# Attention scores on the two row halves of TensorE

## The reference

```
x = x + 0.5 * _L0_ffn_ref(_layernorm(x), ...)
x = x + _L0_attn_ref(_layernorm(x), ...)          # a state-space block
x = x + 0.5 * _L0_ffn_ref(_layernorm(x), ...)
x = x + 0.5 * _L1_ffn_ref(_layernorm(x), ...)     # routed
x = x + _L1_attn_ref(_layernorm(x), ...)          # here
x = x + 0.5 * _L1_ffn_ref(_layernorm(x), ...)

# _L1_attn_ref: NH, NKV = 32, 8 heads of HD = 16
q, k = _apply_rope(q, cos, sin), _apply_rope(k, cos, sin)
k, v = jnp.repeat(k, 4, axis=1), jnp.repeat(v, 4, axis=1)
logits = jnp.einsum('bhqd,bhkd->bhqk', q, k) / 4.0
logits = jnp.where(causal, logits, finfo.min)
out = jnp.einsum('bhqk,bhkd->bhqd', softmax(logits), v)
return out.transpose(0, 2, 1, 3).reshape(...) @ Wo.T
```

## Time and profile before

| | us |
|---|---|
| median of 3 runs | 2516.3 |
| lowest, highest | 2514.64, 2520.89 |
| profiled execution | 2520.89 |
| its span | 2519.0 |
| PE, DVE, ACT, POOL busy | 2371.8, 1661.3, 1313.1, 1329.8 |
| attention in the span | about 2098 to 2453 |
| of it main loop | 2238 to 2440 |

### The profile page before, as it was taken

The page is one execution under the profiler, slowest core; times in us unless marked ns, Lnnn a source line. Parts: engine busy times, 40 slices in busy tenths (PEclk is TensorE's granted clock), DMA queues, the critical chain, the costliest instruction groups (busy, mean ns, idle before and its releaser), DMA issues. The chain is left out here.

```text
span 2519.0 us, 32506 instructions
## 1 busy us (share of the span) xinstructions
PE 2371.8 (94%) x12122; PEld 1833.6 (73%) x12122; DVE 1661.3 (66%) x2163; ACT 1313.1 (52%) x1902; POOL 1329.8 (53%) x875
## 2 busy tenths in 40 slices
PE   6997899999999999999999999999889986989986
PEld 5876688888888888888888888888668753565643
DVE  5555887687588588588578678678365535674424
ACT  2323576477477467467467567567423223325533
POOL 2221498599499499589579679669622200000000
PEclk9998999999999999999999999999889998989997
DMA  4321333233233233233233323323134202000001
GB/s 128 97 80 46 115 110 105 89 96 119 79 111 115 80 104 103 93 100 114 88 102 109 92 89 117 98 95 102 46 84 97 90 14 78 1 2 2 2 1 47
DMA packets 163260, 203.98 MB, mean 81 GB/s; under 512 B 24380, under 2 KB 86080, under 8 KB 162976
## 3 DMA queue, kind: packets, MB, share of 16 engines
q1 hardware_dynamic: 163104, 201.90, 26.3%
HBM read 198.37 MB, written 3.15 MB: 80 GB/s over the span
## 5 line engine op out<-in xcount | busy, mean ns | idle before, releaser
L1892 POOL TENSOR_TENSOR mamba_w_lo<-mamba_raw,mamba_w_hi 128x512 fp32r<-128x512 f32 x272 | 436.1, 1613 | 289.9 <-ACT mamba_w_hi L1720 289.9
L76 PE MATMUL psum<-mamba_hT_lo,mamba_w_hi 128*128 128x512 f32 x1152 | 461.7, 401 | 5.6 <-DVE mamba_bc L1983 3.0
L77 PE MATMUL psum<-mamba_hT_hi,mamba_w_hi 128*128 128x512 f32 x1152 | 456.2, 396 | 0.0
L78 PE MATMUL psum<-mamba_hT_hi,mamba_w_lo 128*128 128x512 f32 x1152 | 456.1, 396 | 0.0
L1911 POOL TENSOR_SCALAR mamba_L<-mamba_A,mamba_ts 128x256 f32<-128x256 f32 (+1 forms) x256 | 334.3, 1320 | 0.1
L2015 DVE TENSOR_TENSOR mamba_L<-mamba_L,mamba_cb 128x1536 f32<-128x1536 f32 x128 | 302.0, 2359 | 22.2 <-ACT mamba_L L1769 16.5
L76 PEld LDWEIGHTS psum<-mamba_hT_lo,mamba_w_hi 128*128 128x128 f32 x1152 | 217.0, 188 | 55.9 <-DVE mamba_bc L1983 3.3
L1983 DVE SCALAR_TENSOR_TENSOR mamba_hid<-psum,mamba_cw,mamba_hid 128x1022 f32<-128x1022 f32 (+2 forms) x192 | 245.1, 1277 | 18.0 <-ACT mamba_hid L1727 13.5
L78 PEld LDWEIGHTS psum<-mamba_hT_hi,mamba_w_lo 128*128 128x128 f32 x1152 | 216.9, 188 | 52.4
L77 PEld LDWEIGHTS psum<-mamba_hT_hi,mamba_w_hi 128*128 128x128 f32 x1152 | 216.9, 188 | 49.1
L2042 DVE SCALAR_TENSOR_TENSOR mamba_zs_lo<-mamba_z,mamba_dgn,mamba_zs_hi 128x512 fp32r<-128x512 f32 x128 | 117.6, 923 | 172.0 <-ACT mamba_zs_hi L1792 172.0
(11 more groups left out here) (278 smaller groups left out, 5002.7 us busy)
## 6 DMA issues: line engine op xcount, KB each, us to landing
mamba_A<-mamba_a_dram SPq DMA_DIRECT2D x128, 512.0 KB, 4.4
mamba_raw<-in_win SPq DMA_DIRECT2D x144, 256.0 KB, 2.6
mamba_raw<-in_wout SPq DMA_DIRECT2D x128, 256.0 KB, 2.6
mamba_Eb<-mamba_e_dram SPq DMA_DIRECT2D x128, 128.0 KB, 3.0
ffn_raw<-in_w SPq DMA_DIRECT2D x80, 128.0 KB, 3.5
ffn_scl<-in_s SPq DMA_DIRECT2D x80, 128.0 KB, 3.7
ffn_scl<-in_s SPq DMA_DIRECT2D x86, 64.0 KB, 2.3
ffn_raw<-in_w SPq DMA_DIRECT2D x20, 256.0 KB, 2.6
```

The lines of the kernel that those rows point to most:

```text
L76: e.matmul(out, wh, ml, start=start, stop=False)
L77: e.matmul(out, wh, mh, start=False, stop=False)
L78: return e.matmul(out, wl, mh, start=False, stop=stop)
L1892: e.tensor_tensor(w.lo[:, k % NSPLIT, :], raw[:, k % NRAW, :], w.hi_read[:, k % NSPLIT, :], ALU.subtract).then_inc(s["w_lo"], 1)
```

## The change

Both score products now contract over 64 rows at a time. `HALVES` names the two halves of the partitions. In `score` the matmul of head h reads rows 64 h to 64 h + 63 of the q stack and of its k stack. The mask is brought in halves too: `halfm[:, n, :]` holds the mask's rows 64 n to 64 n + 63 on both halves of the partitions, and `shifted` is an identity of 64 columns with zeros on both sides, so that a window of 128 columns puts these rows in the right place; four mask matmuls stand where two stood. `score_t(t, m)` computes two key heads, one on each half, into banks 4 and 5, with four mask matmuls of 256 columns on the diagonal, waits until both banks are free, and signals once; units follow in two shares and not in four. Making the new tables takes a memset, a second DMA and three more casts.

```
-                for i in range(4 if t < TQ else 0):
-                    score_t(t, i)
-                    for k in range(i * len(units) // 4, (i + 1) * len(units) // 4):
+                for m in range(2 if t < TQ else 0):
+                    score_t(t, m)
+                    for k in range(m * len(units) // 2, (m + 1) * len(units) // 2):
                         score(*units[k])
```

```
 # score
                     for h in range(2):
-                        e.matmul(psum[:, 2 * (k % 2) + h, 0:n], qs[:, b, z, qt * P:(qt + 1) * P],
-                                 ks[:, b, 2 * (z // QPK) + h, 0:n], start=True, stop=False)
-                    for h in range(2):
-                        last = e.matmul(psum[:, 2 * (k % 2) + h, n - P:n], identr[:], maskr[:], start=False, stop=True)
+                        e.matmul(psum[:, 2 * (k % 2) + h, 0:n], qs[HALVES[h], b, z, qt * P:(qt + 1) * P],
+                                 ks[HALVES[h], b, 2 * (z // QPK) + h, 0:n], start=True, stop=False)
+                    for j in range(2):
+                        for h in range(2):
+                            last = e.matmul(psum[:, 2 * (k % 2) + h, n - P:n],
+                                            shifted[HALVES[h], P // 2 * (1 - j):P // 2 * (1 - j) + P],
+                                            halfm[HALVES[h], j, :], start=False, stop=j == 1)
 # score_t
-                    kv, k = 4 * j + i, 4 * t + i
-                    if k >= 2:
-                        e.wait_ge(exped, k - 1)
+                    k = 4 * t + 2 * m
+                    if k:
+                        e.wait_ge(exped, k)
...
-                    last = e.matmul(out, ks[:, b, kv, kt * P:(kt + 1) * P], q, start=True, stop=kt < qt)
-                    if kt == qt:
-                        last = e.matmul(out, maskr[:], identr[:, :].unsqueeze(1).to_broadcast([P, QPK, P]),
-                                        start=False, stop=True)
+                    for h in range(2):
+                        last = e.matmul(outs[h], ks[HALVES[h], b, 4 * j + 2 * m + h, kt * P:(kt + 1) * P],
+                                        qs[HALVES[h], b, z:z + QPK, qt * P:(qt + 1) * P], start=True, stop=kt < qt)
+                    for n in range(2 if kt == qt else 0):
+                        for h in range(2):
+                            last = e.matmul(outs[h][:, :, HALVES[n]], halfm[HALVES[h], n, :],
+                                            identr[HALVES[h], HALVES[h]].unsqueeze(1).to_broadcast([P // 2, QPK, P // 2]),
+                                            start=False, stop=n == 1)
 # convert (ScalarE)
                 e.wait_ge(sel_cut, 2)
+                e.wait_ge(zeros_set, 1)
...
-                e.copy(maskr[:], cmask[:]).then_inc(mask_ready, 1)
+                e.copy(halfm[:], hmask[:]).then_inc(mask_ready, 1)
                 e.copy(identr[:], ident[:]).then_inc(mask_ready, 1)
+                e.copy(shifted[:], zeros[:]).then_inc(mask_ready, 1)
+                e.wait_ge(mask_ready, 3)
+                for h in HALVES:
+                    e.copy(shifted[h, P // 2:P], ident[h, h]).then_inc(mask_ready, 1)
```

More of the change, by code:

```diff
@@ L842, in attention @@
     ROWS, ONE, SPARE = 32, AHD, 48
+    HALVES = (slice(0, P // 2), slice(P // 2, P))
     SCALE = AHD ** -0.5
@@ L854, in attention @@
         cos, sin, rot = c.sb("cos", [P, SEQ]), c.sb("sin", [P, SEQ]), c.sb("rot", [P, P])
-        cmask = c.sb("cmask", [P, P])
-        maskr, identr = c.sb("maskr", [P, P], F32R), c.sb("identr", [P, P], F32R)
+        hmask = c.sb("hmask", [P, 2, P])
+        identr = c.sb("identr", [P, P], F32R)
+        halfm = c.sb("halfm", [P, 2, P], F32R)
+        shifted = c.sb("shifted", [P, P + P // 2], F32R)
+        zeros = c.sb("zeros", [P, P + P // 2])
         sel = c.sb("sel", [P, 2, QPK + NKV, P], F32R)
-        w_in, sel_in, sel_cut, sel_ready, mask_ready = (c.sem(s) for s in (
-            "w_in", "sel_in", "sel_cut", "sel_ready", "mask_ready"))
+        w_in, sel_in, sel_cut, sel_ready, mask_ready, zeros_set = (c.sem(s) for s in (
+            "w_in", "sel_in", "sel_cut", "sel_ready", "mask_ready", "zeros_set"))
         with ExitStack() as pre:
@@ L872, in cut @@
             def cut(e):
-                e.wait_ge(sel_in, 32)
+                e.memset(zeros[:], 0.0).then_inc(zeros_set, 1)
+                e.wait_ge(sel_in, 48)
                 for half in range(2):
```

14 lines of the change are left out of this document (8 added, 6 removed).

## The result

The changed kernel takes 2533.22 us (median of 7 runs, 2527.85 to 2539.85); the kernel before, on the same chip, 2518.78 us (median of 7). The ratio is 1.0058, with a 95% interval of 1.0046 to 1.0070: about 14.4 us slower, twice the bound of 0.3%. The prediction was 2514.5 us, no measurable difference. The profiled execution took 2539.86 us (span 2538.0) against 2520.89 (2519.0), so the two traces differ by 19 us, more than the medians.

What follows compares the result with a forecast made beforehand. VectorE was taken to bound the first maxima, TensorE's work woven with ScalarE's chain the main loop. Turns -5.4, shape changes +3.3, start +1.1, half clock -0.8 gave -1.8 us from the 2516.3 median: 2514.5 us, range 2508 to 2541.

Steps and rivals of the forecast that it cites:

- The overlap of the halves: Score and mask matmuls: both row halves run beside each other, loads too, so a pair costs what one costs.
- Rivals 1 and 2: Pair loads one behind another, 2540 us, chance 0.15; halves not overlapping at all, 2544 us, chance 0.05.
- The turns: The main loop's 40 turns, from first score load to weighing, summed by type of turn: -5.4 us.
- (a) Shape changes: Scores behind a transpose or output product start later: 22 turns x 0.15 = +3.3 us, between 0 and 6.6.
- (b) The start: Setup ahead of the first projection: extra memset work, mask DMA, casts and copies, +1.1 us, between 0.5 and 1.8.
- (c) Half clock: Stretches at 1.2 GHz in the first maxima and the loop's first turns: together -0.8 us, between -1.6 and +1.
- VectorE idles only at the step's start: First maxima units at half clock: paired units stay under VectorE's 1.13 us, so -1.1 us.
- rival 3: TensorE, with less to do, falls to 1.2 GHz in the main loop: up to 2575 us, or 2530; chance 0.06.
- Because ScalarE, which now gets two banks at once and gives both back at once, is late next: Main loop: the reason given for turns saving only 5.4 us of the 38 us of TensorE time taken away.

Runs made afterwards that it cites:

- e6: The change plus overwritten score pairs in the 40 turns only, nothing added in the first 32 maxima units: 2519.89 us, ratio 1.0002.
- e9: The change with the turns' score pairs in four banks, a third of the units behind the weighing, setup casts on VectorE: 2504.90 us, ratio 0.9948.
- e10: The same as e9, but with the full-row matmuls of the kernel before, no halves anywhere: 2521.51 us, ratio 1.0015.
- e8: The kernel before, full rows, without the two mask matmuls in each of the first 32 maxima units: 2520.50 us, ratio 1.0003.
- e11: The change with a semaphore making the lower half's score wait for the upper half's in the first 32 units: 2541.97 us, ratio 1.0093.
- e4_serial: The change with one half's three matmuls listed ahead of the other's in the first 32 units: 2532.55 us, ratio 1.0057.
- e7: The kernel before plus one overwritten 512-column score matmul ahead of each of its first 32 maxima units: 2519.19 us, ratio 0.9998.

## Why the prediction was wrong, step by step

**The overlap of the halves: right.** A pair costs what one costs (0.49 us), the halves start 3 to 4 ns apart, and loads overlap too. Rivals 1 and 2 did not happen.

**The turns: right in kind and nearly in size.** From the first score to the weighing, forecast and measured at full clock: 384 columns 2.50 and 2.45, on the diagonal 2.97 and 2.93 (second pair 1.92 us after the first, as said); 256 columns 2.44 and 2.40, 2.78 and 2.74, on the diagonal 3.25 and 3.22; 128 columns 2.76 and 2.78 or 2.73, on the diagonal 3.23 and 3.21. The sum by these is about -6.8 us where the forecast had -5.4. The diagonal turn at 384 columns (L1065 the mask), beside the earlier trace rows:

```profile
2275.44 0.50 PE L1061 MATMUL psum<-attn_qs,attn_ks 64*128 64x512 f32 x2
2275.77 0.40 PE L1065 MATMUL psum<-attn_identr,attn_halfm 64*128 64x256 f32 x4
...
2277.36 0.50 PE L1061 MATMUL psum<-attn_qs,attn_ks 64*128 64x512 f32 x2 [0.83 <-ACT attn_hT L1184]
...
2278.37 0.64 PE L1077 MATMUL psum<-attn_hT,attn_v 128*32 128x512 f32 x4
```

**(a) Shape changes: right in kind, too small in size.** The score behind an output transpose starts 0.58 us after it instead of 0.41, with the idle of 0.17 us that was forecast:

```profile
2266.41 0.65 PE L1091 MATMUL psum<-s_ident,attn_og 128*128 128x128 f32 x4 [0.71 <-ACT attn_og L1190]
2266.99 0.19 PEld L1061 LDWEIGHTS psum<-attn_qs,attn_ks 64*128 64x128 f32 x2 [0.17 <-issue]
```

That is one turn. Over all turns the term was +3.3 (between 0 and 6.6). In the 37 turns that are at 1.00 throughout both before and in e6 (whose fill doesn't lengthen a turn), the weighing starts 7.1 us sooner in sum, counted from the first score, and 6.0 us are lost between the weighing and the next turn's first score: 0.12 to 0.18 at most of the places where a transpose or a product stands between, but 0.30 at two of them and 0.50 at three. The net is -1.1 us where the prediction had -2.1 (-5.4 + 3.3), so the halves gain next to nothing at full clock.

**(b) The start: right.** +1.0 us against +1.1. ScalarE's casts and TensorE's wait for them, which was 1.51 us:

```profile
2113.45 0.40 ACT L892 CAST attn_halfm<-attn_hmask 128x256 fp32r<-128x256 f32 x1
2113.75 0.29 ACT L893 CAST attn_identr<-s_ident 128x128 fp32r<-128x128 f32 x1
2113.95 0.35 ACT L895 CAST attn_shifted<-attn_zeros 128x192 fp32r<-128x192 f32 x1
2114.33 0.51 ACT L898 CAST attn_shifted<-s_ident 64x64 fp32r<-64x64 f32 x2
2115.59 3.46 PE L221 MATMUL psum<-s_ident,attn_xn 128*128 128x128 f32 x16 [2.54 <-ACT attn_hT L212]
```

**(c) Half clock: this is the step that failed.** "Together -0.8 (between -1.6 and +1)" took the share of half clock as given and asked only what a unit costs in it. Time at half clock went from 20 to 85 us of the two stages: +15 us in the turns by the price above (and the 13 turns that it touches are 13.8 us longer in sum), and +1.1 instead of -1.1 in the first units. There "VectorE idles only at the step's start" was wrong as well. At half clock the scores of successive units start 1.13 and 1.31 us apart in turn, so every other maximum of 1.13 us comes 0.18 late:

```profile
2228.73 0.79 PE L1034 MATMUL psum<-attn_ks,attn_qs 64*128 64x512 f32 x2
...
2230.04 0.80 PE L1034 MATMUL psum<-attn_ks,attn_qs 64*128 64x512 f32 x2 [0.19 <-DVE attn_mx L1247]
...
2231.17 0.79 PE L1034 MATMUL psum<-attn_ks,attn_qs 64*128 64x512 f32 x2
```

The price of a turn at half clock was foreseen in rival 3 (+0.86 for the weighing, measured +0.87), and rival 3 is what happened, in 49 of the turns' 229 us; it had a chance of 0.06. The evidence that I held against it was "from 2198 to 2217, with waits between all units, the granted clock stays 1.00". The very next row said 0.83 for the same kind of unit. The clock falls before at 2216.9 and at 2237.4, both times while TensorE waits for the last maximum of a step (idle 1.37 and 1.33 us ahead of L1029); the 0.95 of 2238 to 2298 is the rest of the second fall. And the waits in that row are not those of the changed kernel: TensorE idles 0.23 us between units there, and 0.46 in the changed kernel at full clock. A change that takes 38 us of TensorE's work out of these stages, and leaves each remaining matmul half of its rows, had to be asked what it does to the clock first. The Trainium skill (TensorE: Matmul & The Clock Gate, What's actually happening) describes the clock as released by TensorE's own activity; the windows of e6 agree (0.80 to 0.92 and 0.95 to 1.00 with more work). I had used that rule for no term.

**"Because ScalarE, which now gets two banks at once and gives both back at once, is late next": right**, and e9 and e10 prove it: with two more banks the halves bring what they did not bring in the change. The Trainium skill (TensorEngine Tiling, PSUM Bottleneck) says that tiling makes TensorE faster but not the evacuation of PSUM; here the trace agrees, with 0.83 us of idle ahead of the second pair.

The medians differ by 14.4 us and the profiles by 19, of which 3.2 lie ahead of the attention. The share of half clock moves from one execution to the next: the mean granted clock of the whole execution was 0.958 to 0.964 in the 26 executions of the changed kernel, and 0.971 to 0.976 in those of the kernel before in all rounds. The fastest of the 26 (2527.85 us) had 0.964, the slowest (2539.86, the profiled one) 0.958. So the profile after is from the end with most half clock, and the medians' difference is the better number for the cost. Open: what exactly makes the clock fall, and whether the halves lower it beyond the work that they take away.

## What to carry to other kernels

Before you take work from TensorE, ask what the granted clock of the stretch will do: less work there can cost more than it saves (here 0.42 us for each us at half clock). A fall nearby is a warning (0.83 next to the loop), but a clock of 1.00 is no safety: 2412 to 2440 had 1.00 before and 0.76 after. An overwritten matmul in an idle gap tells in one run whether it is the clock. Packing two matmuls into one pays only if what takes their results keeps up: free the consumer first (more banks, work moved between), and only then pack. The same packing cost 14 us in the kernel before and was worth 17 us in the one with four banks.

## What the runs showed of the hardware that I had not expected

- Less work for TensorE can mean less clock even where it is busy most of the time: without two masks of 128 columns in a unit (e8) 21.6 us of the first units were at half clock instead of 7.4. With 64-row scores one behind another (e11), as many columns in a unit but longer units, it was 52.4 us; how much of that the halves do themselves is open.
- Matmuls on different row halves need not run in the order of the list: in e4_serial the two halves' scores started 10 ns apart, though two masks of the first half stand between them in the list (first mask 0.59 us later). The Trainium skill (TensorE: Matmul & The Clock Gate, The mechanism) says that matmuls are strictly in order in start and end; with row halves this trace differs, and the measurement decides. The increment of the semaphore was on the last matmul of the list, which also ended last.
- The half clock at the loop's start can come from the stretch ahead of it: in the kernel before the clock falls at 2237.4, in a wait of 1.33 us ahead of the loop, stays down 6.2 us into it, and is 1.00 for the next 196 us. Entered at full clock (e7), the loop has no half clock, and the last stage is 3.5 us shorter in the profile.
- VectorE can make 128x3072 and the small casts in time that it idles: the attention's first score came 3.4 us sooner in e9 and 3.7 in e10.
